# A gather that waits for the block before: a graph and LSTM kernel on one Trainium2 core

## What is computed

```python
t = layernorm(x)
agg = segment_sum(t[src], dst, 6250)
h = relu((t + agg) @ W1 + b1)
x1 = x + relu(h @ W2 + b2)
# then an LSTM over the 6250 rows of layernorm(x1), one sequence
y = x1 + lstm(layernorm(x1), W_f, W_i, W_c, W_o, b_f, b_i, b_c, b_o)
```

## Time and profile before

| | |
|---|---|
| Runs | 2987.83, 2981.14, 2975.06 us; median 2981.14 |
| Profiled execution, span from first to last instruction | 2970.5 us |
| The profiled execution's own time | given as its span alone; the runs lie 4.6 to 17.3 us above it |
| Busy in the span | PE 2593.4 us, DVE 2147.9, ACT 1564.9, POOL 1009.0 |
| Gathers L811 | 800, 836.7 us on POOL |
| Granted TensorE clock, mean | 0.940 |

### The profile page before, as it was taken

The page is one execution under the profiler, slowest core; times in us unless marked ns, Lnnn a source line. Parts: engine busy times, 40 slices in busy tenths (PEclk is TensorE's granted clock), DMA queues, the critical chain, the costliest instruction groups (busy, mean ns, idle before and its releaser), DMA issues. The chain is left out here.

```text
span 2970.5 us, 47617 instructions
## 1 busy us (share of the span) xinstructions
PE 2593.4 (87%) x10746; PEld 1893.3 (64%) x10747; DVE 2147.9 (72%) x5785; ACT 1564.9 (53%) x3986; POOL 1009.0 (34%) x1018
## 2 busy tenths in 40 slices
PE   7966988878889888898888799899999799989997
PEld 6844766657667666676666566666666455655554
DVE  7745766767777677676676588777777777768886
ACT  5643444444444444444443566566656576757775
POOL 0236656655666566565653100000000000013333
PEclk9978999989999998899989899999999899999998
DMA  9657776767777777677766776577777666569995
GB/s 239 182 146 210 209 218 202 221 198 208 220 220 220 214 214 214 197 217 211 216 205 199 194 190 169 173 241 239 237 241 236 169 171 171 166 158 251 252 253 142
DMA packets 194202, 611.09 MB, mean 206 GB/s; under 512 B 41822, under 2 KB 47966, under 8 KB 164394
## 3 DMA queue, kind: packets, MB, share of 16 engines
q1 hardware_dynamic: 120432, 370.08, 42.0%
q0 software_dynamic: 73712, 240.39, 29.6%
HBM read 468.71 MB, written 141.62 MB: 205 GB/s over the span
## 5 line engine op out<-in xcount | busy, mean ns | idle before, releaser
L811 POOL DMA_INDIRECT kept<-ln_table,kept x800 | 836.7, 1046 | 554.7 <-DVE shared L1014 307.6
L1502 PE MATMUL acc<-shared,state 128*125 128x512 f32 x2244 | 775.0, 416 | 62.8 <-DVE state L1798 47.3
L851 ACT ACTIVATE shared<-kept 128x512 fp32r<-128x512 f32 x800 | 449.3, 626 | 403.7 <-remote 223.3
L1502 PEld LDWEIGHTS acc<-shared,state 128*125 128x125 f32 x2244 | 401.2, 187 | 198.9 <-ACT acc L1433 66.1
L904 PE MATMUL agg<-shared,onehot 128*125 128x512 f32 x1200 | 433.4, 463 | 33.0 <-DVE shared L1014 17.3
L1343 POOL TENSOR_TENSOR out<-h,lx 125x512 f32<-125x512 f32 x50 | 64.5, 1289 | 1122.6 <-DVE h L1823 1122.6
L904 PEld LDWEIGHTS agg<-shared,onehot 128*125 128x125 f32 x1200 | 254.1, 220 | 104.5 <-issue 37.1
L1502 PE MATMUL acc<-W_low,state 128*125 128x512 f32 x800 | 316.5, 396 | 0.0
L1502 PE MATMUL acc<-last_high,state 128*125 128x512 f32 x748 | 298.6, 399 | 0.0
L1014 DVE TENSOR_TENSOR shared<-kept,shared 128x512 fp32r<-128x512 f32 x400 | 267.1, 687 | 14.8 <-ACT shared L851 7.6
L924 PE MATMUL gps<-Wx_high,zT_high 128*125 128x512 f32 x800 | 226.0, 405 | 39.6 <-ACT zT_high L886 33.7
(11 more groups left out here) (235 smaller groups left out, 4295.4 us busy)
## 6 DMA issues: line engine op xcount, KB each, us to landing
xg<-total_rows SPq DMA_DIRECT2D x100, 896.0 KB
xg<-gate_rows SPq DMA_DIRECT2D x88, 896.0 KB
gate_rows<-gout SPq DMA_DIRECT2D x200, 224.0 KB
total_rows<-total SPq DMA_DIRECT2D x50, 896.0 KB
kept<-ln_table,kept POOLq DMA_INDIRECT x800
lx<-x_rows POOLq DMA_DIRECT2D x50, 250.0 KB, 7.3
out_dram<-out POOLq DMA_DIRECT2D x50, 250.0 KB, 2.9
held<-in_x_dram SPq DMA_DIRECT2D x25, 448.0 KB
```

The costliest lines, as they stand in the source:

```text
L811: e.indirect_dma_start(out=rows[j % RING][:, :], out_offset=None, in_=table[:, :], in_offset=bass.IndirectOffsetOnAxis(ap=ends[:, b, j, 0: ...
L851: e.activation(high[j % PARTS][:, :], rows[j % RING][:, :], ACT.Copy).then_inc(s_high, 1)
L1502: m = e.matmul(acc[n][0:L, :], stationary[:, k, :], weights[k][:, n * PAIR:(n + 1) * PAIR], start=begins, stop=(k == K - 1), skip_group_ch ...
```

## The change

POOL's gather 12 of block b (b over 0) waits for `s_hin` to reach b, which is hin of block b-1. The register loads are split: each engine loads one number where it needs one, and POOL reuses the number of extra columns that it has.

```diff
-        def range_of(e, b):
-            _, (before, extra, begin) = nc.values_load_multi_w_load_instructions(
-                ranges[0:1, bass.ds(b, 1), 0:3].rearrange("o b n -> o (b n)"), engines=[e.engine],
...
+        def extra_of(e, b):
+            _, (extra,) = nc.values_load_multi_w_load_instructions(
+                ranges[0:1, bass.ds(b, 1), 1:2].rearrange("o b n -> o (b n)"), engines=[e.engine],
...
+        def begin_of(e, b):
+            _, (begin,) = nc.values_load_multi_w_load_instructions(
+                ranges[0:1, bass.ds(b, 1), 2:3].rearrange("o b n -> o (b n)"), engines=[e.engine],
...
+        def before_of(e, b):
+            _, (before,) = nc.values_load_multi_w_load_instructions(
+                ranges[0:1, bass.ds(b, 1), 0:1].rearrange("o b n -> o (b n)"), engines=[e.engine],
...
+        REST_AT = 12
...
             def beyond(b):
-                before, extra, begin = range_of(e, b)
+                extra = extra_of(e, b)
                 with e.If(extra > 0):
+                    before = before_of(e, b)
                     with e.Fori(0, extra) as g:
-                        visit(before + g, g, begin)
+                        visit(before + g)
...
             def load_ends(b):
-                begin = range_of(e, b)[2]
+                begin = begin_of(e, b)
...
             def gather(n, b, j):
                 if j == 0:
                     hold(e, s_passed, s_ends, b * 16 + 16)
+                if j == REST_AT and b > 0:
+                    e.wait_ge(s_hin, b)
                 e.wait_ge(s_low, n + 1)
...
                 with e.If(extras[b % CHECKED] > 0):
-                    before, extra, begin = range_of(e, b)
+                    extra, begin = extras[b % CHECKED], begin_of(e, b)
+                    before = before_of(e, b)
                     with e.Fori(0, extra) as g:
                         gather_beyond(before + g, g, begin)
```

More of the change, by code:

```diff
@@ L725, in no_columns @@
             pass
-        def range_of(e, b):
-            _, (before, extra, begin) = nc.values_load_multi_w_load_instructions(
-                ranges[0:1, bass.ds(b, 1), 0:3].rearrange("o b n -> o (b n)"), engines=[e.engine],
-                min_val=0, max_val=E, skip_runtime_bounds_check_because="the first part bounds it")
-            extra = nc.s_assert_within(extra, 0, MOST, skip_runtime_bounds_check_because="the first part bounds it")
-            begin = nc.s_assert_within(begin, 0, E, skip_runtime_bounds_check_because="the first part bounds it")
-            return before, extra, begin
+        def extra_of(e, b):
+            _, (extra,) = nc.values_load_multi_w_load_instructions(
+                ranges[0:1, bass.ds(b, 1), 1:2].rearrange("o b n -> o (b n)"), engines=[e.engine],
+                min_val=0, max_val=MOST, skip_runtime_bounds_check_because="the first part bounds it")
+            return extra
+        def begin_of(e, b):
+            _, (begin,) = nc.values_load_multi_w_load_instructions(
+                ranges[0:1, bass.ds(b, 1), 2:3].rearrange("o b n -> o (b n)"), engines=[e.engine],
+                min_val=0, max_val=E, skip_runtime_bounds_check_because="the first part bounds it")
+            return begin
+        def before_of(e, b):
+            _, (before,) = nc.values_load_multi_w_load_instructions(
+                ranges[0:1, bass.ds(b, 1), 0:1].rearrange("o b n -> o (b n)"), engines=[e.engine],
+                min_val=0, max_val=BLOCKS * MOST)
+            return before
         CHECKED = 5
+        REST_AT = 12
         def extras_of(e, b):
@@ L851, in high_part, with high_beyond @@
                 e.activation(high[j % PARTS][:, :], rows[j % RING][:, :], ACT.Copy).then_inc(s_high, 1)
-            def high_beyond(n, g, begin):
+            def high_beyond(n):
                 hold(e, s_passed, s_go_x, n + 1)
@@ L906, in visit, with visit_beyond @@
                 m.then_inc(s_visit, 1)
-            def visit_beyond(n, g, begin):
+            def visit_beyond(n):
                 e.wait_ge(s_hot_x, n + 2)
@@ L1015, in low_of_rows, with beyond_columns @@
                                 high[j % PARTS][:, :].bitcast(F32), ALU.subtract).then_inc(s_low, 1)
-            def beyond_columns(n, g, begin):
+            def beyond_columns(n):
                 e.wait_ge(s_visit_x, n + 1)
```

## The result

The changed kernel takes 3094.11 us (median of four runs, 3081.31 to 3097.38), the kernel before 2983.32 us on the same chip (four runs, 2975.06 to 2987.83): ratio 1.0382, 95% interval 1.0358 to 1.0407. 3077 us was forecast. The profiled execution took 3081.31 us, 13 under the median, and its span is 3079.7.

What follows compares the result with a forecast made beforehand. No engine is full; PE's increments, held during POOL's gather bursts, make hin wait. Steps of 30.65 against 28.46 us give +105, the start -9: +96, span 3066.5, plus 10.6 to the median: 3077 us, range 2930 to 3215.

Steps and rivals of the forecast that it cites:

- PE's 24.3 us a step: Graph part: PE's busy time per step, taken as the nearest floor under the 28.46 us step.
- start: POOL's gathers behind each hin: the run begins 1.0 us after it, 0.69 for hin and 0.3 of queue.
- run: POOL, graph part: one burst of 16 gathers behind each hin, 20.3 us long.
- release: From the end of the last gather to zT_high on ACT: 2.9 us.
- from zT_high to the next hin: Rest of the graph step, without an extra column: 6.45 us.
- the case of the earlier trace: Two earlier bursts of 16 gathers on POOL took 20.0 and 21.7 us; 20.3 was taken, nearer the first.
- Rival B: Second layer of the graph step: late is caught in the burst too, 33.2 us a step, 3200 us; chance 0.20.
- some 40 waits of zT_high: Sign in the changed profile: ACT's zT_high waits for remote rise from 7 to some 40, about 8 us each.
- Start: Ahead of the first hin: POOL issues 28 gathers in place of 35, -9 us.
- F: Graph step: z's increment slips through during the burst, so faster, 2821 or 2724 us; chance 0.22.
- N: Graph step: increments are late for reasons other than gather order, so it stays 28.5 us, 2981 in all; chance 0.08.
- theory one: Experiments' claim: PE increments due while POOL issues indirect DMAs are held until that run ends, unless early in it.

Runs made afterwards that it cites:

- plain rows: Changed kernel without its hold, POOL's gathers replaced by plain row loads on ACT's queue: 3700.03 us (23.00 a step), kernel before 2987.05.
- the change on chip 3: The changed kernel itself run again on another chip, against the kernel before there: 3059.72 beside 2959.56 us, ratio 1.035.
- half rows: Changed kernel without its hold, each gather from block 1 on fetching 1 KB in place of 2: 2975.6 us, kernel before 2987.05.
- three or four: Changed kernel with POOL's gathers cut by waits into 5, 5, 6 (2906.15 us, 0.983), or 6, 6, 4 with its hold moved (2910.44 us, 0.985).
- the hold on late: Changed kernel with gather 12 waiting for s_late in place of s_hin: 2901.79 us, kernel before 2696.19 on the same chip.
- the stop for z: Changed kernel plus gather 8 waiting for the transpose of z of block b-2: 2693.81 us (0.999) on chip 2, 2874.19 us (0.971) on chip 12.
- four stops: Changed kernel with its hold moved to gather 10 behind hin's transpose, plus waits at gathers 0 (late) and 6 (z's transpose): 2910.44 us, 0.985.

## Why the prediction was right, and where its sizes were off

*What bounds it.* The reading of the earlier trace rows held: with no gathers (plain rows) a step is 23.0 us on average and no wait for "remote" is left. PE's 24.3 us a step, though, are no floor: they were measured at a mean granted clock of 0.91, and on chip 2 at 1.00 the step is 22.3 us. The hold took hin's wait away as the prediction said, 25.5 us left against "under 30".

*The sum.* In the step shown: start 0.96 us (1.0 forecast), run 21.30 (20.3), release 2.25 (2.9), from zT_high to the next hin 5.85 (6.45); together 30.36 against 30.65. The run was mis-sized by one microsecond, since some of its gathers take 1.1 to 1.5 us (mean 1046 ns, nearer to the case of the earlier trace rows than to that of the earlier trace rows which I took); two terms that were too large by 0.6 each made up for it, which is luck.

*The mechanism, and how far it goes.* Long runs of gathers delay what comes from PE, and the step follows: that was right. But the forecast had z transposed in time and seen late in every step. That is so in 14 of 48. In the others late is caught, or PE itself falls behind, and that these cost about the same (30.3 to 32.5 us with a run of 16) was not foreseen. To that degree the close mean is luck.

*Rival B was not a rival but a part.* I put late's capture as a case for all steps or none. It comes in 21 of 48 steps, at 31.68 us on average and at most 32.87, not 33.2. That is one reason why the mean is 30.85 and not 30.4; against the 30.65 forecast it makes 48 x 0.2 = 10 of the 17 us between forecast and median. The start makes 1.0 of the rest, what lies behind the last step 2.7, and the distance from span to median, 14.4 in place of 10.6, the last 3.8.

*Which increment.* Forecast were some 40 waits of zT_high of 8 us. There are 15 for "remote", of 7.3 on average; counting all releasers, 24 are over 2 us. In the other 16 runs of 16 it is not z's increment that is late but PE. The timelines of ACT, PE and POOL in the step from 1399.46 to 1431.67:

```profile
1414.09 0.63 ACT L866 ACTIVATE shared<-kept 128x512 fp32r<-128x512 f32 x1 [8.20 <-remote]
...
1416.17 0.72 ACT L897 ACTIVATE between<-between,grs 125x512 f32<-125x512 f32 x1 [0.74 <-issue]
...
1419.79 0.40 PE L939 MATMUL gps<-Wx_high,zT_low 128*125 128x512 f32 x1 [2.46 <-issue]
1421.93 0.37 PE L933 MATMUL z_turned<-ident,between 125*128 125x125 f32 x1 [1.74 <-issue]
1423.35 0.86 PE L933 MATMUL z_turned<-ident,between 125*128 125x125 f32 x3 [1.05 <-issue]
...
1419.50 0.95 POOL L825 DMA_INDIRECT kept<-ln_table,kept  x1 [0.30 <-issue]
```

ACT stands for the visits' increment first and gets it while POOL still gathers. It has written z by 1416.89, but PE, without a wait that the profile shows, stands 2.46, 1.74 and 1.05 us between its instructions. The run ends at 1420.45, the transposes at 1424.21. Over the 16 steps z was written 16.0 to 20.3 us behind hin and the last transpose ended at 23.0 to 25.2. So PE's work ends a little behind the run as z's increment does in the first kind, and the price was nearly right with the wrong name on half of it. The change on chip 3 shows the same: 16 of its 29 runs of 16 are of the second kind. Whether PE stops because its increments are not let go, or both have another cause, no run here tells.

*Start, loads, clock.* -8.0 us against -9; nothing to 7 us for the loads against nothing; 0.89 for the clock against "below 0.91".

*Rivals F and N.* F needed z to be held under 6.2 us; in the step shown ACT used it 7.75 us behind the end of the transposes. N fell with half rows and plain rows. The Trainium skill (SBUF — State Buffer, "Who interferes with whom") says that PE and ACT never wait on anyone. It says so of the ports of SBUF, so the forecast was no fair test of it, and chip 2 agrees with it: no such wait is seen there. For semaphores on the other chips the measurement decides: PE's result is there and its increment is not seen, as in the step with late, for 10 us.

## What to carry to other kernels

Before you move POOL's indirect DMAs out of the way of one wait, list every increment of PE's that another engine waits for, and PE's own work too, and lay the moved run over all of them. Moving the run moves the wait; shortening it at the point where the next increment is due takes most of it away, and here one stop placed so (0.971) was better than three or four (0.983 and 0.985). And take the kernel before on the same chip beside every run: what is tuned here is a property of some chips.

## What was not expected of the hardware

- One chip of the four numbered ones showed no held increments at all: 22.3 us a step with unbroken gathers, 2696 us in place of 2960 to 2987. On it the stops are worth nothing (0.999 and 1.004), and the hold on late costs 7.6%.
- z's increment is let go 1.6 to 2.5 us behind the end of a run of sixteen in the changed kernel, 0.9 to 1.7 us behind one of twelve in the kernel with the stop for z. Late's mostly comes before the run is over, so theory one is too strict where it says that an increment is held to the end. Why they differ is open, and so is why a given increment passes in one step and is caught in the next at the same place: late, due about 8 us behind hin, is used between +7.7 and +18.1 in the changed kernel (but for one step behind an extra column).
- PE does not only seem late, it stands still within the runs: 53.8 us at the transposes of z in the changed kernel. In the kernel with four stops its four transposes of z, the later ones of which wait for nothing, stand 2.5 us apart between the second and the third (1024.11 and 1026.91 us). On chip 2 and with plain rows it does not. No run here tells why.
